# Expert weights for a mixture-of-experts tile loop: read from HBM tile by tile instead of copied on the chip

## The reference

```python
h = _layernorm(x, axis=-1) * (1 + ca) + sa
x = x + ga * attention(h)            # layer 0: retention with a gate; layer 1: causal softmax
h = _layernorm(x, axis=-1) * (1 + cb) + sb
x = x + gb * ffn(h)                  # 8 experts, each token goes to its top 2

# layer 0 expert:  relu(h @ W1[e] + b1[e]) @ W2[e] + b2[e]          W1 128x512, W2 512x128, fp32
# layer 1 expert: (silu(h @ gate[e].T) * (h @ up[e].T)) @ down[e].T  three matrices of 128x512, fp32
```

## Time and profile before

| | before |
|---|---|
| median of 3 runs | 704.83 us |
| span of the profiled execution, first to last instruction | 747.2 us |
| busy: TensorE / VectorE / ScalarE / GpSimd | 503.5 / 386.2 / 262.4 / 337.1 us |
| moved by DMA | 61.94 MB |
| mean granted TensorE clock, share of 2.4 GHz | 0.811 |

### The profile page before, as it was taken

One profiled execution on the slowest core, in us unless ns is written; L12 is line 12 of the kernel. 1 busy time (PEld: TensorE's weight loads), 2 busy tenths in 40 slices (PEclk: granted clock), 3 DMA queues, 4 the chain that ended last, 5 costly groups with the idle time before them and its releaser, 6 DMA issues.

```text
span 747.2 us, 13354 instructions
## 1 busy us (share of the span) xinstructions
PE 503.5 (67%) x4221; PEld 401.7 (54%) x4221; DVE 386.2 (52%) x996; ACT 262.4 (35%) x639; POOL 337.1 (45%) x425
## 2 busy tenths in 40 slices
PE   6384878563277687773369977969831678878870
PEld 5263655452177586762346555545420578878770
DVE  5373977464934344444487554644227534434335
ACT  1221223111044334432125543535600455545442
POOL 2731545233156555654324432636731355555543
PEclk9686878765578979895589988989955699999995
DMA  6667564612011111112564545432221011111116
GB/s 187 148 177 151 138 165 139 158 35 63 1 36 44 39 35 42 39 40 86 160 159 101 111 112 99 124 81 50 60 53 36 22 39 36 39 38 36 35 33 168
DMA packets 67649, 61.94 MB, mean 83 GB/s; under 512 B 9792, under 2 KB 59456, under 8 KB 66048
## 3 DMA queue, kind: packets, MB, share of 16 engines
q1 hardware_dynamic: 50128, 40.05, 21.4%
q10 hardware_dynamic: 12480, 11.04, 5.4%
q0 software_dynamic: 4992, 10.23, 4.5%
HBM read 44.19 MB, written 17.10 MB: 82 GB/s over the span
## 4 chain that ended last, share of the span: by engine, by line
PE 34%; DMA 16%; issue 12%; DVE 12%; SPq 8%; another core or an unknown queue 6%; POOL 5%; ACT 4%; ACTq 1%; DVEq 1%; POOLq 0%
PE bank L797 11%; PE pair L808 6%; DMA max_d<-qk 5%; DMA stack_k<-parts_d 4%; PE pair L797 3%; SPq L454 2%; DMA parts_d<-parts 2%; SPq L433 2%; PE bank L875 2%; PE bank L604 2%; SPq L438 2%; PE pair L861 1%; DMA probs<-h_d,src_row 1%; PE pair L841 1%
## 5 line engine op out<-in xcount | busy, mean ns | idle before, releaser
L797 PE MATMUL bank<-probs,stack_q 128*128 128x128 f32 x708 | 103.7, 296 | 41.8 <-ACT probs L1443 21.0
L1669 POOL DMA_INDIRECT ye_d<-probs,dst_row x78 | 78.3, 1004 | 95.9 <-DVE probs L1217 45.3
L797 PEld LDWEIGHTS bank<-probs,stack_q 128*128 128x128 f32 x708 | 93.2, 207 | 48.9 <-issue 22.7
L1663 POOL DMA_INDIRECT probs<-h_d,src_row x78 | 75.9, 974 | 38.3 <-issue 20.4
L808 PE MATMUL pair<-qk,stack_k 128*128 128x128 f32 x624 | 89.8, 290 | 3.3 <-DVE stack_k L1225 3.1
L808 PEld LDWEIGHTS pair<-qk,stack_k 128*128 128x128 f32 x624 | 81.8, 204 | 6.4 <-issue 5.8
L1717 POOL TENSOR_SCALAR_AFFINE_SELECT probs<-probs 128x256 f32<-128x256 f32 (+1 forms) x96 | 46.4, 487 | 76.3 <-ACT probs L1534 75.7
L1534 ACT ACTIVATE probs<-pair 128x512 f32<-128x512 f32 x96 | 56.6, 598 | 50.0 <-PE pair L861 49.3
L1204 DVE COPY qk<-W 128x512 f32 x78 | 37.4, 479 | 49.2 <-issue 26.3
L875 PE MATMUL bank<-probs,V 128*32 128x256 f32 (+1 forms) x512 | 52.0, 337 | 4.1 <-POOL probs L1717 3.9
L841 PE MATMUL pair<-stack_k,stack_q 96*128 96x128 bf16 (+1 forms) x256 | 41.7, 273 | 17.8 <-DMA stack_k<-parts_d 11.1
(11 more groups left out here) (194 smaller groups left out, 992.7 us busy)
## 6 DMA issues: line engine op xcount, KB each, us to landing
parts_d<-parts SPq DMA_DIRECT2D x16, 384.0 KB, 3.9
W<-in_w ACTq DMA_DIRECT2D x16, 256.0 KB, 3.8
stack_q<-parts_d SPq DMA_DIRECT2D x16, 192.0 KB
stack_k<-parts_d SPq DMA_DIRECT2D x16, 192.0 KB
mod_bc<-mod_d SPq DMA_DIRECT2D x16, 192.0 KB, 6.0
W_up<-in_up_w ACTq DMA_DIRECT2D x8, 256.0 KB, 4.6
stack_q<-parts_d SPq DMA_DIRECT2D x16, 128.0 KB
stack_k<-parts_d SPq DMA_DIRECT2D x16, 128.0 KB
```

Of the source, the lines that this page charges most:

```text
L797: i = pe.matmul(at[r % 2][:, k * P:(k + 1) * P], w_now[:, r % 2, which, k * P:(k + 1) * P], x_t[:, r % 2, :], start=True, stop=True)
L1663: gp.indirect_dma_start(out=x_rows[:, n % RING, :], out_offset=None, in_=h_d[l], in_offset=bass.IndirectOffsetOnAxis(ap=src_row[:, n:n + 1 ...
L1669: gp.indirect_dma_start(out=ye_d[l], out_offset=bass.IndirectOffsetOnAxis(ap=dst_row[:, n:n + 1], axis=0), in_=y_rows[:, n % RING, :], in_ ...
```

## The change

The weights are no longer kept in SBUF. In its tile loops SyncE reads, for each tile, the expert's number and issues the DMAs from HBM of that expert's matrices: two in layer 0, three in layer 1. They go into a ring of four tiles. The copies of matrices on ScalarE and VectorE are gone, the bias copies stay. The loads of all experts during attention are gone. The hardware loop is gone too: all 39 tiles are written out on each engine. The second matrix lies in HBM in the order of the SBUF rows now, so that one partition's part is one run of 2 KB instead of four of 512 bytes. Two semaphores are merged, by which TensorE's first projection of layer 0 waits for `rotary` as well.

```diff
+            def load_weights(l):
+                first, up, second_w = (("w1", None, "w2"), ("gate_w", "up_w", "down_w"))[l]
+                sp.wait_ge(sem[f"tile_exp{l}"], base[f"tile_exp{l}"] + 1)
+                for n in range(TILES):
+                    r = n % RING
+                    e = sp.value_load(tile_exp[0:1, n:n + 1], min_val=0, max_val=E - 1)
+                    at_least(sp, sem[f"hidden_ps{l}"], n - RING + 1, base[f"hidden_ps{l}"])
+                    sp.dma_start(w_now[:, r, 0, :], ins[first][bass.ds(e, 1), :, :].rearrange("a p f -> p (a f)"))\
+                      .then_inc(sem[f"w_in{r}_{l}"], 16)
+                    if up is not None:
+                        at_least(sp, sem["up_ps"], n - RING + 1)
+                        sp.dma_start(w_now[:, r, 1, :], ins[up][bass.ds(e, 1), :, :].rearrange("a p f -> p (a f)"))\
+                          .then_inc(sem[f"w_in{r}_{l}"], 16)
+                    at_least(sp, sem[f"y_ps{l}"], n - RING + 1, base[f"y_ps{l}"])
+                    sp.dma_start(w2_now[:, r], ins[second_w][bass.ds(e, 1), :, :].rearrange("a p f -> p (a f)"))\
+                      .then_inc(sem[f"w_in{r}_{l}"], 16)
...
-    with eng.Fori(0, TURNS) as i:
-        for u in range(PEEL, PEEL + RING):
-            step(i * RING + u, u % RING, i + u // RING)
-    for n in range(TILES - RING, TILES):
+    for n in range(TILES):
         step(n, n % RING, n // RING)
...
                 def first(n, r):
                     pe.wait_ge(sem[f"x_t{l}"], base[f"x_t{l}"] + n + 1)
-                    pe.wait_ge(sem[f"w_now{l}"], base[f"w_now{l}"] + 2 * n + 2)
+                    pe.wait_ge(sem[f"w_in{r}_{l}"], base[f"w_in{r}_{l}"] + 16 * (l + 2) * (n // RING + 1))
...
                 def second(n, r):
-                    pe.wait_ge(sem[f"w2_now{l}"], base[f"w2_now{l}"] + (n + 1) * (2 - l))
...
-                    ve.tensor_copy(w2_now[:, r % 2], W2[:, bass.ds(e, 1), :, :].rearrange("p e k c -> p (e k) c"))\
-                      .then_inc(sem[f"w2_now{l}"], 1)
...
-                        act.copy(w_now[:, r % 2, 0, :], W1[:, bass.ds(e, 1), :].rearrange("p e f -> p (e f)"))\
-                           .then_inc(sem["w_now1"], 1)
-                        act.copy(w_now[:, r % 2, 1, :], W_up[:, bass.ds(e, 1), :].rearrange("p e f -> p (e f)"))\
-                           .then_inc(sem["w_now1"], 1)
...
-                if a is not None:
-                    load_expert(0, a)
...
-                if 0 <= s - 1 < E:
-                    load_expert(1, s - 1)
```

More of the change, by code:

```diff
@@ L117 @@
     **dict.fromkeys(("x_t", "x_t_e_ps", "hidden_ps", "act_hid", "hid_t", "y_ps", "y_rows"), TILES),
-    "w_now": 2 * TILES, "w2_now": 2 * TILES,
+    "b_now": TILES, "b2_now": TILES,
     **{f"{way}{r}": 16 * ((TILES - r + RING - 1) // RING) for way in ("gathered", "scattered") for r in range(RING)},
+    **{f"w_in{r}": 32 * ((TILES - r + RING - 1) // RING) for r in range(RING)},
     **dict.fromkeys(("ranks_ps", "counts_ps", "total_b", "picked_b", "tiles_before_b", "src_row", "dst_row", "tile_exp",
@@ L130, in exists, with all_tiles @@
 def exists(n):
[L132 to L138, removed]
-    with eng.Fori(0, TURNS) as i:
-        for u in range(PEEL, PEEL + RING):
-            step(i * RING + u, u % RING, i + u // RING)
-    for n in range(TILES - RING, TILES):
+    return 0 <= n < TILES
+def all_tiles(step):
+    for n in range(TILES):
         step(n, n % RING, n // RING)
@@ L167, in at_least @@
 def at_least(eng, sem, count, base=0):
-    if not isinstance(count, int) or count > 0:
+    if count > 0:
         eng.wait_ge(sem, count + base)
@@ L796, in first @@
                             at = banks if l == 1 or k < FK // 2 else UP
-                            i = pe.matmul(at[r % 2][:, k * P:(k + 1) * P], w_now[:, r % 2, which, k * P:(k + 1) * P],
+                            i = pe.matmul(at[r % 2][:, k * P:(k + 1) * P], w_now[:, r, which, k * P:(k + 1) * P],
                                           x_t[:, r % 2, :], start=True, stop=True)
@@ L819, in expert_tiles @@
                 transpose_rows(0, 0, 0)
-                all_tiles(pe, step)
+                all_tiles(step)
                 second(TILES - 1, (TILES - 1) % RING)
@@ L1235, in step @@
                         at_least(ve, sem["y_rows0"], n)
-                    if exists(n + 1):
+                    if l == 0 and exists(n + 1):
                         copy_second(n + 1, r + 1)
-                ve.wait_ge(sem[f"tile_exp{l}"], base[f"tile_exp{l}"] + 1)
-                ve.wait_ge(sem[f"experts{l}_in"], 16 * (2 * E + 2 * (l == 0)))
-                copy_second(0, 0)
-                all_tiles(ve, step)
+                if l == 0:
+                    ve.wait_ge(sem["tile_exp0"], 1)
+                    ve.wait_ge(sem["experts0_in"], 32)
+                    copy_second(0, 0)
+                all_tiles(step)
                 keep_rows(TILES - 1, (TILES - 1) % RING, (TILES - 1) // RING)
@@ L1475, in step @@
                         keep_x_t(n + 1, r + 1)
-                    if exists(n + 2):
+                    if l == 0 and exists(n + 2):
                         copy_first(n + 2, (r + 2) % RING, e)
-                act.wait_ge(sem[f"tile_exp{l}"], base[f"tile_exp{l}"] + 1)
-                act.wait_ge(sem[f"experts{l}_in"], 16 * (2 * E + 2 * (l == 0)))
-                if l == 1:
-                    act.wait_ge(sem["up_in"], 16 * E)
+                if l == 0:
+                    act.wait_ge(sem["tile_exp0"], 1)
+                    act.wait_ge(sem["experts0_in"], 32)
                 for n in range(2):
-                    copy_first(n, n, expert_of(n))
+                    if l == 0:
+                        copy_first(n, n, expert_of(n))
                     if n == 0:
                         keep_x_t(0, 0)
-                all_tiles(act, step)
+                all_tiles(step)
             def gap_exp_of(l):
@@ L1777 @@
         "up_w": a["L1_ffn_up_w"].transpose(0, 2, 1),
-        "down_w": a["L1_ffn_down_w"].transpose(0, 2, 1),
+        "down_w": a["L1_ffn_down_w"].transpose(0, 2, 1).reshape(E, FK, P, C).transpose(0, 2, 1, 3).reshape(E, P, FK * C),
     }
```

68 lines of the change are left out of this document (27 added, 41 removed).

## The result

| kernel | median of the runs | ratio to before, 95% interval |
|---|---|---|
| before, same group of runs | 703.5 us (20 runs) | 1 |
| changed | 708.3 us (20 runs) | 1.0085 [1.0064, 1.0107] |

The change makes the kernel slower by 0.85%, about 6 us. The forecast was 696, 9 us faster.

What follows compares the result with a forecast made beforehand. TensorE was taken to bound layer 1's loop, VectorE and GpSimd almost equally layer 0's. Layer 0's loop -7, attention -4.5, rate +1, starts +1.5 gave -9 us: 696 us, range of 8 in 10 684 to 717.

Steps and rivals of the forecast that it cites:

- layer 0's loop: Layer 0's tile loop: without VectorE's matrix copies GpSimd bounds it at 2.57 us per tile; -7 us, bounds 0 to -9.
- the written-out code has more instructions to fetch, a few per cent of the bytes; nothing: All written-out tiles: fetching the longer code was costed at nothing.
- The trace doesn't agree: Hardware loop's jumps: transposes across two of them are 2.79 and 2.81 us apart, against the skill's rule that taken branches stall.
- Some 2 us longer costs nothing within the loops: Gathers in both tile loops: issued about 7 us before their transpose, so landing some 2 us later costs nothing.
- Starts, +1.5: Start of each tile loop: first gather delayed beside a flood of weight loads; +0.75 us per layer, bounds 0 and +5.
- Attention, -4.5: Attention, both layers: expert loads leave, so TensorE waits less for stack loads; -4.5 us, bounds 0 and -19.
- Layer 1's rate, +1: Layer 1's tile loop: weights and gathers need 329 GB/s, at the edge of the DMA rate; +1 us, +21 at 274 GB/s.
- SyncE: SyncE's issue of weight loads in both loops: 1.9 us of layer 1's 2.79 per tile, 1.5 of layer 0's 2.57; fits.
- Rival 2: Layer 1's loop: DMA becomes the bound, TensorE waiting for weights at each tile; 711 us (707 to 725), chance 0.28.
- side remark on late gathers: Rival 2's addition: gathers that come late beside full queues could add 5 us.
- The unnamed waits: Tile loops: 42.6 us of waits with unnamed releaser, read as added by the profiler and taken off the loops' lengths.
- rival 1: Tile loops: the unnamed waits are real, from the hardware loop, and writing it out removes them; 654 us, chance 0.12.

Runs made afterwards that it cites:

- written_out: Kernel before with all 39 tiles written out, copies and attention's loads kept: 707.1 us, ratio 1.0062 to before.
- after_looped: Changed kernel with hardware loop back on TensorE, VectorE, ScalarE, SyncE: 703.0 us, ratio 0.9997 to before; on 752 kind 755.0 and 753.3 us.
- pe_looped: Changed kernel with the hardware loop put back on TensorE alone: 704.0 us, ratio 1.0027 to before.
- pe_written: Changed kernel with the hardware loop on VectorE, ScalarE and SyncE, TensorE's tiles written out: 708.7 us, ratio 1.0094 to before.
- before, second profile: Trace of the unchanged kernel before from run `before_third`, on a chip of the 703 kind: span 701.1 us.
- fill_once: Changed kernel reading weights only for each layer's first four tiles, later tiles computing with those: 700.9 us, ratio 0.9954 to before.
- gather_ahead8: Changed kernel with gathered rows in a ring of eight instead of four, eight gathers issued at each start: 697.7 us, ratio 0.9911 to before.
- attn_loads: Changed kernel with expert loads during attention put back as traffic only: 715.2 us, ratio 1.0158 to before.
- before_third: Kernel before, unchanged, run again on a chip of the 703 kind: 703.7 us, ratio 1.0012.
- written_ahead8: Kernel before with all tiles written out, copies kept, ring of eight gathered tiles, on a 752 chip: 746.1 us, ratio 0.9904 to before.
- before_again: Kernel before, unchanged, run again on a chip of the 752 kind: 752.1 us, ratio 0.999, span 749.3.
- late_weights: Changed kernel with weights of tile 1 and later held until the first gather lands: 754.2 us (ratio 1.0009), on 703 kind 709.1 (1.010).

## Why the prediction was wrong

**Two steps made the forecast wrong: layer 0's loop, worked out at -7 us and not there (below), and "the written-out code has more instructions to fetch, a few per cent of the bytes; nothing".** Without the first the forecast would have been -2 us; the second is what made the change a loss. As to the second step, the bytes are few indeed: eight packets of 16 KB in layer 1's loop beside 30 MB of weights. But each takes 0.9 to 1.3 us of one DMA engine, and a gather is complete only when all its rows have landed. Measured: +4.4 us beside copies (`written_out`), +6.2 beside streams (changed kernel against `after_looped`), of which 4.1 are TensorE's code (`pe_looped`); the other 2 lie within the intervals. That this code is the cause is shown by `pe_looped` and `pe_written`. That it costs by way of gathers, and not by TensorE running short of code, shows in TensorE's idle time after the first transpose of the two loops: 24.1 us in the changed kernel, of which 21.0 end with a gather and the rest, but for 0.3, with ScalarE or VectorE; with the loop put back 18.2, of which 14.6 end with a gather. That a single packet delays a gather shows best in `written_out`, where no streams blur it: of the six transposes of layer 0's loop that come over 3.1 us after the one before, five (226.9, 244.8, 263.3, 279.6 and 298.5) come 2 to 3 us after one of its five q8 packets. That trace has all landings: the five gathers in flight beside such a packet took 3.2 to 4.0 us, the other 34 a median of 2.6. Here are the last of the five and the queues from 295 to 299:

```profile
294.43 0.97 POOL L1658 DMA_INDIRECT probs<-h_d,src_row  x1 [0.30 <-issue]
298.46 0.33 PE L779 MATMUL bank<-consts,probs 128*128 128x128 f32 x1 [1.80 <-DMA probs<-h_d,src_row]
```
```profile
q8 instruction: 1, 0.02, 1.9%
```

Which engine held which row is not in the trace.

The Trainium skill (Runtime: NRT & Kernel Launch, Instruction fetch mechanics) has an engine's code refilled in blocks of 16 KiB, at a cost that is mostly hidden. The packets of q8 have that size. For TensorE's own instructions the trace agrees: but for the 0.3 us above, nothing could be a wait for code. For the kernel it does not: what the fetch hides from TensorE it puts on a gather. The same section says that a taken branch to code outside the fetched window stalls, and gives this as one reason why kernels prefer full unrolling. Here the looped form is the faster one, by 0.9%. In before, second profile, no packet of q8 comes between 591.7 and 671.2, from the second turn of layer 1's hardware loop to its end: its code was not fetched again for each turn. So the rule's condition was not met, and the prediction's "The trace doesn't agree" tested nothing of it.

**"Some 2 us longer costs nothing within the loops": wrong.** The step took a gather's lead, the time from its issue to its transpose, as 7 us. That fits layer 1 of the trace it was read from (median 6.8), but layer 0 has 4.1 there. In before, second profile, it is 5.2 us in layer 1 and 2.6 in layer 0, which is the landing time itself: GpSimd is the bound there, and issues each gather only just before its use. With the streams layer 0 has 4.0. An even delay should cost that once a loop, not per tile (in `after_looped` layer 0's loop is 1.3 us longer); an uneven one, such as the 6.3 us above, runs into GpSimd's next scatters. From first transpose to last scatter, in us, each of one profiled execution:

| kernel | layer 0 | layer 1 |
|---|---|---|
| before, second profile | 104.1 | 112.7 |
| `written_out` | 105.5 | 113.4 |
| `fill_once` | 102.9 | 113.3 |
| changed | 107.7 | 118.1 |
| `after_looped` | 105.4 | 115.2 |
| `pe_looped` | 104.0 | 115.7 |
| `pe_written` | 104.8 | 117.4 |
| `gather_ahead8` | 97.0 | 114.6 |

`fill_once`, written out but without copies or streams, stays near before (-1.2 and +0.6 us); it suggests that written-out code costs little when nothing else is beside it, but a looped form of it was not run. The streams alone, in the looped form, cost 1.3 + 2.5 us.

**Layer 0's loop, -7: not there, the largest miss of the sum.** The new loop was worked out as 103.5 us, and before's as 112.4 after the unnamed waits were taken off. On a chip without these waits before takes 104.1: its loop was already at GpSimd's 2.57 us per tile (median of its scatters' distances). VectorE's 2.68 of the earlier trace rows was a single tile; in before, second profile, the median distance of its matrix copies in layer 0 is 2.56. The rate of the bound was right, and the length of what it replaced was wrong.

**Starts, +1.5: mis-sized.** In `after_looped` against before, second profile, 4.81 less 2.77 and 4.11 less 2.54 us: +3.6. Within the bound of 5.

**Attention, -4.5: right in size, not in place.** `attn_loads` gives 5.1. By the traces the first gather of layer 0 comes at 202.3 instead of 205.3, and that of layer 1 249.8 instead of 251.8 us after layer 0's last scatter (means of the eight profiles on chips of the 703 kind without expert loads in attention, and of `before_third` and `written_out`): 3.0 + 2.0. The wait of the earlier trace rows did not shrink in the changed kernel; it comes 3.4 us earlier.

**Layer 1's rate, +1, and SyncE: right in the mechanism.** Layer 1's loop grew by 2.5 us in the looped form instead of 1, but not by its rate. Transposes at 2.79 us with a DMA share of 0.94; a load takes SyncE 0.33 to 0.38 us to issue, with single ones up to 1.45, and no load of weights stands among TensorE's waits in the loop. Rival 2 gave a price near the measured one (711) for a reason that did not come: its mark, TensorE waiting for weights at each tile, is absent. Only its side remark on late gathers holds. That layer 1's copies were worth nothing was right too: 113.3 us without them and without streams (`fill_once`), 112.7 with them.

The Trainium skill (DMA: Bandwidth & Descriptors, Queues, rings and completion order) has an engine take turns between queues by packets. The median gather of layer 0 takes 4.0 us beside the streams and 2.6 without, and the one beside the 16 KB packet 6.3, which fits such a rule but does not test it: how the packets of the queues followed each other on one engine is not in the trace.

**The unnamed waits.** The forecast took them off, rightly, but put them down to the profiler; rival 1 put them down to the hardware loop. Both were wrong. A kernel with no such loop has them on a chip of the 752 kind (`written_ahead8`), and before has none in a profile on the other kind. Why TensorE's results come late on some chips stays open.

**The sum.** With what the traces of `after_looped` and the medians show: +1.3 (layer 0) + 2.5 (layer 1) + 3.6 (starts) - 5.1 (attention) + 6.2 (written-out code) = +8.5 us, where 6.0 were measured. The first three terms are differences of two single profiles, of which `after_looped`'s lies 2.1 us above its median and before's 0.9 below: if all of that lies in these terms, they are some 3 us too large together, and 8.5 less 3 is 5.5. Term by term the forecast of -9 missed by 8.3 (layer 0's loop), 6.2 (written-out code), 2.1 (starts) and 1.5 (layer 1) less 0.6 (attention), 17.5 us, where 15 were measured.

## What to carry over

Look at how far ahead of its use a latency-bound transfer is issued before filling the DMA engines beside it: here each gather of layer 0 went out exactly as late as it could, and gathers that took 1 to 3 us longer, at the loops' starts and within them, took back the 5 us that the change had won in attention and more. Count code as traffic too where such a transfer has no slack; here a hardware loop of four tiles took the cost away, and with a lead of eight gathers TensorE waited for none of them. And before taking a wait off as an artefact, profile the same kernel on a second chip.

## What the runs showed of the hardware that was not expected

- Two kinds of chips, 703 and 752 us for one kernel at nearly the same mean granted clock (0.824 in `before_third`, 0.812 in `before_again`). The whole difference lies in the tile loops, where ScalarE and VectorE stand idle for up to 5.7 us before TensorE's results reach them. The granted clock in layer 0's loop is lower there too, 0.88 against 0.97; whether as a cause or as a result of the waits is open. On the slower kind the looped form of the changed kernel and `late_weights` stay within 0.4% of before; the changed kernel itself was not timed there.
- One 16 KB packet of TensorE's code about every 14 us of layer 1's written-out tiles (changed kernel: 575, 590, 605, 619, 633, 647 and 662), each 0.9 to 1.3 us of one DMA engine; with TensorE's hardware loop of four tiles none from the second turn to its end.
- A gather's way from issue to transpose: in layer 0's loop 2.6 us in before, second profile, at a DMA share of 0.16, 4.0 in the changed kernel at 0.75, and 6.3 for one beside a packet of code. A scatter's landing rose in the same way, from 2.3 to 3.6 us in layer 0's loop (the changed kernel's trace has it for 10 of the 39).
